# A smooth-quantised stage in halves: column maxima and factor rows read from PSUM, shifts on ScalarE, weights scaled by VectorE, the residual added by GpSimd

## The reference

```python
def _smooth_quant_linear(x, w):
    amax_x = jnp.max(jnp.abs(x), axis=0)
    amax_w = jnp.max(jnp.abs(w), axis=0)
    s = jnp.sqrt(jnp.maximum(amax_x, EPS) / jnp.maximum(amax_w, EPS))
    s = jnp.maximum(s, EPS)
    xs = x / s
    ws = w * s
    x_scale = jnp.maximum(jnp.max(jnp.abs(xs), axis=-1, keepdims=True), EPS) / QMAX
    w_scale = jnp.maximum(jnp.max(jnp.abs(ws), axis=-1, keepdims=True), EPS) / QMAX
    x_q = jnp.clip(jnp.round(xs / x_scale), -QMAX, QMAX)
    w_q = jnp.clip(jnp.round(ws / w_scale), -QMAX, QMAX)
    return x_q @ w_q.T * x_scale * w_scale.T

def _expert_forward(xe, guw, dw):
    h = _smooth_quant_linear(xe, guw)
    gate, up = jnp.split(h, 2, axis=-1)
    a = jax.nn.silu(gate) * up
    return _smooth_quant_linear(a, dw)
```

## Time and profile before

| | us |
|---|---|
| median of 3 runs | 1110.71 |
| lowest, highest | 1105.49, 1112.2 |
| profiled execution, time | 1110.76 |
| profiled execution, span | 1109.0 |
| PE busy in the span | 850.5 (77%) |
| DVE busy | 741.6 (67%) |
| ACT busy | 567.9 (51%) |
| POOL busy | 406.2 (37%) |

### The profile page before, as it was taken

How to read it: one execution, slowest core, us unless ns; L and a number is a source line. 1 busy time by engine, 2 the same in 40 slices (tenths; PEclk the granted TensorE clock), 3 DMA queues, 4 the chain that set the end, 5 groups by cost and what they waited for, 6 DMA issues and landing times. The chain is left out here.

```text
span 1109.0 us, 16326 instructions
## 1 busy us (share of the span) xinstructions
PE 850.5 (77%) x5170; PEld 503.2 (45%) x5170; DVE 741.6 (67%) x1441; ACT 567.9 (51%) x1070; POOL 406.2 (37%) x332
## 2 busy tenths in 40 slices
PE   3356666979899999998597588998539999634477
PEld 1122223642477777776376452332416666422135
DVE  5799996879666676666788557994533333157785
ACT  3433342477677777776474365887304432123162
POOL 0476650047555555553231270000025665202122
PEclk8689998999999999999699597999759999856589
DMA  3222205600000000000000101400572333230001
GB/s 91 78 76 76 76 1 199 219 10 11 10 15 19 19 20 20 14 19 1 5 1 1 52 1 39 135 3 2 201 276 53 74 49 48 28 96 0 0 1 38
DMA packets 44330, 57.61 MB, mean 52 GB/s; under 512 B 5656, under 2 KB 35104, under 8 KB 44272
## 3 DMA queue, kind: packets, MB, share of 16 engines
q1 hardware_dynamic: 37776, 48.72, 13.1%
q0 software_dynamic: 4416, 6.03, 3.3%
q10 hardware_dynamic: 2080, 2.10, 0.5%
HBM read 50.29 MB, written 6.49 MB: 51 GB/s over the span
## 5 line engine op out<-in xcount | busy, mean ns | idle before, releaser
L1225 POOL TENSOR_TENSOR a_scratch<-a_scratch,a_inverse 128x512 f32<-128x512 f32 x64 | 66.6, 1041 | 117.8 <-DVE a_inverse L1357 117.8
L322 PE MATMUL bank<-ssm_seen,ident 128*128 128x512 f32 x128 | 63.6, 621 | 39.0 <-DVE ssm_seen L498 39.0
L424 POOL TENSOR_TENSOR ssm_drive<-ssm_du,ssm_b_row 128x1024 f32<-128x1024 f32 x32 | 75.2, 2352 | 33.4 <-DVE ssm_state L488 33.3
L2204 DVE TENSOR_REDUCE a_tops<-bank 128x4 f32<-128x1024 f32 x64 | 77.6, 1223 | 13.5 <-PE bank L1893 10.7
L2403 PE MATMUL bank<-wup,moe_xT 128*128 x184 | 84.9, 605 | 1.2 <-ACT moe_xT L2461 1.1
L390 ACT ACTIVATE bank<-ssm_delta,ssm_a_neg 128x510 f32<-128x510 f32 x64 | 44.1, 690 | 80.7 <-DVE ssm_state L488 77.7
L2633 DVE TENSOR_TENSOR moe_act_f<-bank,moe_silu 128x512 f32<-128x512 f32 x23 | 15.9, 692 | 96.0 <-ACT moe_silu L2468 84.2
L488 DVE TENSOR_TENSOR_SCAN ssm_state<-bank,ssm_drive 128x512 f32<-128x512 f32 x64 | 74.8, 1210 | 7.6 <-POOL ssm_drive L424 4.9
L2057 ACT ACTIVATE wup<-bank,a_exp_scale 128x1024 f32<-128x1024 f32 x64 | 71.1, 1114 | 16.9 <-PE bank L1916 16.8
L1144 ACT ACTIVATE a_scratch<-bank,a_bias,a_q_factor 128x256 f32<-128x256 f32 x128 | 71.1, 560 | 10.4 <-DVE a_bias L1344 10.1
L969 PE MATMUL bank<-keys,a_scratch 128*128 (+1 forms) x256 | 69.8, 396 | 0.7 <-DVE keys L1282 0.4
(11 more groups left out here) (477 smaller groups left out, 2190.4 us busy)
## 6 DMA issues: line engine op xcount, KB each, us to landing
ssm_b_row<-ssm_b_spill SPq DMA_DIRECT2D x16, 512.0 KB, 3.6
wup<-in_l_up_dram SPq DMA_DIRECT2D x8, 1024.0 KB, 8.6
a_wq_in<-in_l1x_q_dram SPq DMA_DIRECT2D x32, 128.0 KB, 2.1
wdn<-in_l_down_dram SPq DMA_DIRECT2D x8, 512.0 KB, 9.6
keys<-in_l1x_o_dram SPq DMA_DIRECT2D x1, 2048.0 KB, 12.7
X<-in_x_dram SPq DMA_DIRECT2D x1, 1024.0 KB
lora_raw<-in_l_gate_dram SPq DMA_DIRECT2D x1, 1024.0 KB, 8.3
lora_raw<-in_l_up_dram SPq DMA_DIRECT2D x1, 1024.0 KB, 10.3
```

Source lines behind the costliest of these rows:

```text
L322: last = pe.matmul(bank[:, 4 + 2 * k + h, :], core.ident[:, :], seen[:, k, h * HALF:(h + 1) * HALF], start=False, stop=m >= STEPS - CC, sk ...
L424: pool.tensor_tensor(drive[:, k, :], du[:, k, :], b_row[:, n % NROW, :], ALU.mult).then_inc(S["drive_ready"], 1)
L1225: pool.tensor_tensor(prob[:, j, :, :], prob[:, j, :, :], inverse[:, j, :].unsqueeze(2).to_broadcast([P, 2, SEQ]), ALU.mult).then_inc(S["p_ ...
L2204: dve.tensor_reduce(tops[:, f // 2 % 3, :, first:first + 2].rearrange("p q h -> p h q"), bank[:, at:at + 2, :].rearrange("p h (q n) -> p h ...
```

## The change

The whole stage goes by halves of four tiles (`tiles(h)`). The column maxima are read from PSUM, where TensorE turned the activations, and ScalarE no longer makes `xnT`. The spread factor rows are not copied to SBUF: VectorE reads them from PSUM as it multiplies (`rows`). Each spread matmul starts after its own four diagonals. VectorE multiplies the weights too, in place of GpSimd. Multiplying by the inverse scale and adding 1.5 * 2^23 is done by ScalarE, one instruction per tile with two per-partition factors (`shifted`); all roundings to integers are VectorE's, by halves, set between its other steps. The weights' scale row comes in two halves: the first ahead of the turned weights, the second behind products 0 and 1; ScalarE multiplies it by the gate in the second product. Of the first product's turned weights VectorE copies one of the two chunks. Silu, its product, its turning and the second maxima go by halves, and the two table loads of ScalarE are placed by hand. In the second product VectorE writes the rescaled tile to `hidden`, and GpSimd adds it to `X`. In the diff, lines taken out are left out where the listing above has them.

```diff
@@ declarations @@
...
+        shift = s.sb("shift", [P, 1])
-        rows = lambda r, row: row[:, :, :].unsqueeze(2).to_broadcast([P, NB, 2, wide(r)])
+        tiles = lambda h: slice(NT // 2 * h, NT // 2 * (h + 1))
+        def rows(r, first, h):
+            flat = bank[:, first + h, :] if r == 0 else bank[:, first, h * SEQ:(h + 1) * SEQ]
+            return flat.rearrange("p (b n) -> p b n", b=2).unsqueeze(2).to_broadcast([P, 2, 2, wide(r)])
...
@@ -2739,84 +2742,106 @@
             @block.tensor
             def _(pe):
                 s.norm_tensor(pe)
...
+                def spread(r, first, factors, ready, count):
+                    for h in range(CHUNKS[r]):
+                        pe.wait_ge(ready, count + h + 1)
+                        pe.matmul(bank[:, first + h, :], core.ones[:, :], factors[:, 4 * h:4 * h + 4, :],
+                                  start=True, stop=True).then_inc(row_s[r], 1)
+                def turn_ints(r, ints, dst, banks, h):
+                    pe.wait_ge(ints[r], h + 1)
+                    for c in range(CHUNKS[r]):
+                        for t in range(NT // 2 * h, NT // 2 * (h + 1)):
+                            last = pe.transpose(half_bf(banks[r][c])[:, t * P:(t + 1) * P],
+                                                dst[r][:, t, c * P:(c + 1) * P], core.identh[:, :])
+                    return last
+                def scale_row(r, h):
+                    pe.wait_ge(diag_w[r], h + 1)
+                    pe.matmul(bank[:, 2 + h, :], core.ones[:, :], diag[:, 4 * h:4 * h + 4, :], start=True, stop=True
+                              ).then_inc(row_w[r], 1)
+                def multiply(r, t):
+                    if t >= 2:
+                        pe.wait_ge(used[r], t - 1)
+                    for c in range(CHUNKS[r]):
+                        last = pe.matmul(bank[:, t % 2, 0:DM], xqT[r][:, c, t * P:(t + 1) * P],
+                                         wqT[r][:, c, t // 2 * DM:(t // 2 + 1) * DM], start=c == 0, stop=c == CHUNKS[r] - 1)
+                    last.then_inc(product[r], 1)
                 def quantised(r):
                     C = CHUNKS[r]
...
+                    spread(r, 2, diag_inv, diag_s[r], 0)
+                    spread(r, 0, diag, diag_s[r], C)
                     for h in range(2):
...
+                        last = turn_ints(r, x_int, xq, XB, h)
+                    last.then_inc(x_turned[r], 1)
+                    scale_row(r, 0)
+                    for h in range(2):
+                        last = turn_ints(r, w_int, wq, WB, h)
+                    last.then_inc(w_turned[r], 1)
                     pe.wait_ge(x_back[r], 1)
...
+                    pe.wait_ge(w_back[r], C)
+                    multiply(r, 0)
+                    multiply(r, 1)
+                    scale_row(r, 1)
+                    for t in range(2, NT):
+                        multiply(r, t)
                 quantised(0)
...
+                for h in range(2):
+                    pe.wait_ge(a_ready, h + 1)
+                    for t in range(4):
+                        last = pe.transpose(bank[:, 4 + h, t * P:(t + 1) * P], a_nat[:, 4 * h + t, :], core.ident[:, :])
+                    last.then_inc(a_turned, 1)
                 quantised(1)
             @block.scalar
             def _(act):
...
+                s.norm_root(act)
+                def shifted(nat, mult, ready, done, h):
+                    act.wait_ge(ready, h + 1)
+                    for t in range(NT // 2 * h, NT // 2 * (h + 1)):
+                        last = act.activation(nat[:, t, :], nat[:, t, :], ACT.Identity, scale=mult[:, t:t + 1], bias=shift[:, 0:1])
+                    last.then_inc(done, 1)
+                def scale_row(r, h):
+                    act.wait_ge(row_w[r], h + 1)
+                    act.activation(w_scale_row[r][:, h * HALF:(h + 1) * HALF], bank[:, 2 + h, :], ACT.Copy,
+                                   scale=1.0 if r == 0 else gate).then_inc(rowcopy_w[r], 1)
                 def quantised(r):
...
                     act.wait_ge(ratio[r], 1)
                     act.activation(smooth[r][:, :], amax_x[r][:, :], ACT.Sqrt).then_inc(root[r], 1)
...
+                    for h in range(2):
+                        shifted(x_nat[r], x_mult[r], x_scaled[r], x_shifted[r], h)
+                    for h in range(2):
+                        shifted(w_nat[r], w_mult[r], w_scaled[r], w_shifted[r], h)
                     act.wait_ge(x_turned[r], 1)
                     act.copy(xqT[r][:, :, :], half_bf_banks(XB[r])).then_inc(x_back[r], 1)
+                    scale_row(r, 0)
                     act.wait_ge(w_turned[r], 1)
...
+                    act.copy(wqT[r][:, 0, :], half_bf(WB[r][0])).then_inc(w_back[r], 1)
+                    scale_row(r, 1)
                 half_bf_banks = lambda bs: bank[:, bs[0]:bs[-1] + 1, :].bitcast(BF16)
+                act.wait_ge(shift_ready, 1)
                 quantised(0)
...
+                act.preload_act_table_set("silu_and_others")
+                for h in range(2):
+                    act.wait_ge(used[0], NT // 2 * (h + 1))
+                    act.activation(silu[:, tiles(h), :], hidden[:, tiles(h), 0:CTX], ACT.Silu).then_inc(silu_done, 1)
+                act.preload_act_table_set("sqrt_and_others")
                 quantised(1)
             @block.gpsimd
             def _(pool):
...
+                pool.memset(shift[:, :], ROUND).then_inc(shift_ready, 1)
+                for t in range(NT):
+                    pool.wait_ge(used[1], t + 1)
+                    pool.tensor_tensor(core.X[:, t, :], core.X[:, t, :], hidden[:, t, :], ALU.add).then_inc(times, 1)
             @block.vector
             def _(dve):
@@ -2828,69 +2853,82 @@
                     ins.then_inc(step, 1)
                     dve.wait_ge(step, steps[0])
...
+                def diagonals(dst, blocks, column):
+                    for k in blocks:
                         last = dve.tensor_scalar(dst[:, k, :], core.ident[:, :], column(k), None, ALU.mult)
                     return last
...
+                def scale_part(r, first, nat, scale, mult, done, count, h):
+                    dve.wait_ge(row_s[r], count + min(h, CHUNKS[r] - 1) + 1)
+                    chain(dve.tensor_tensor(shape(nat[:, tiles(h), :]), shape(nat[:, tiles(h), :]), rows(r, first, h), ALU.mult))
+                    chain(dve.tensor_reduce(scale[:, tiles(h)], nat[:, tiles(h), :], AX.X, ALU.max, apply_absolute_value=True))
+                    chain(dve.tensor_scalar(scale[:, tiles(h)], scale[:, tiles(h)], EPS, 1.0 / QMAX, ALU.max, ALU.mult))
+                    dve.reciprocal(mult[:, tiles(h)], scale[:, tiles(h)]).then_inc(done, 1)
+                def integers(nat, shifted, dst, done, h):
+                    dve.wait_ge(shifted, h + 1)
+                    dve.tensor_scalar(dst[:, tiles(h), :], nat[:, tiles(h), :], ROUND, QMAX, ALU.subtract, ALU.min).then_inc(done, 1)
+                def quantised(r):
                     C = CHUNKS[r]
...
                     chain(dve.tensor_scalar(amax_x[r][:, :], amax_x[r][:, :], EPS, None, ALU.max))
                     dve.tensor_tensor(amax_x[r][:, :], amax_x[r][:, :], amax_w[r][:, :], ALU.mult).then_inc(ratio[r], 1)
                     dve.wait_ge(root[r], 1)
                     chain(dve.tensor_scalar(smooth[r][:, :], smooth[r][:, :], EPS, None, ALU.max))
...
                     chain(dve.reciprocal(inverse[r][:, :], smooth[r][:, :]))
                     at = lambda k: slice((k % C) * NB + k // C, (k % C) * NB + k // C + 1)
...
+                    for dst, values in ((diag_inv, inverse[r]), (diag, smooth[r])):
+                        for h in range(C):
+                            diagonals(dst, range(4 * h, 4 * h + 4), lambda k: values[:, at(k)]).then_inc(diag_s[r], 1)
+                    x = lambda h: scale_part(r, 2, x_nat[r], x_scale[r], x_mult[r], x_scaled[r], 0, h)
+                    w = lambda h: scale_part(r, 0, w_nat[r], w_scale[r], w_mult[r], w_scaled[r], C, h)
+                    x(0)
+                    x(1)
+                    dve.wait_ge((w_in, c_in)[r], 16)
+                    w(0)
+                    integers(x_nat[r], x_shifted[r], xq[r], x_int[r], 0)
+                    w(1)
+                    integers(x_nat[r], x_shifted[r], xq[r], x_int[r], 1)
+                    dve.wait_ge(w_scaled[r], 2)
+                    for h in range(2):
+                        diagonals(diag, range(4 * h, 4 * h + 4), lambda k: w_scale[r][:, k:k + 1]).then_inc(diag_w[r], 1)
+                        integers(w_nat[r], w_shifted[r], wq[r], w_int[r], h)
+                    if C == 2:
+                        dve.wait_ge(w_turned[r], 1)
+                        dve.tensor_copy(wqT[r][:, 1, :], half_bf(WB[r][1])).then_inc(w_back[r], 1)
+                def rescale(r, t):
                     dve.wait_ge(product[r], t + 1)
...
+                    dve.wait_ge(rowcopy_w[r], t // 4 + 1)
```

(23 more changed lines are left out.)

110 lines of the change are left out of this document (5 added, 105 removed).

## The result

The changed kernel takes 1097.22 us (median of 4, 1093.48 to 1104.49) against 1110.38 us; the ratio of its runs to those of before is 0.9886, 95% interval 0.9841 to 0.9931. Timed again twice it came to 0.9861 (0.9819 to 0.9903) and 0.9853 (0.9826 to 0.9879). Over all series of runs, 16 executions of it have a mean of 1096.4 us and 56 of the kernel before 1111.0 us: 14.6 us less, with a standard error of 1.1. The kernel before timed against itself gave 1.0018 (0.9996 to 1.0039). The forecast was 1097.8 us.

What follows compares the result with a forecast made beforehand. VectorE was taken to lead the last stage, its idle quarter being hand-offs between engines. Gains 1.94, 6.47, 2.1, 4.0 and 0.45 less a 2.0 loss summed to 13.0 us, from 1110.76 to 1097.8 us; range 1092 to 1105.

Steps and rivals of the forecast that it cites:

- maxima from PSUM: First product: four VectorE maxima read PSUM directly, ending at 985.07 us where the maximum ended at 987.01; gain 1.94 us.
- to the first rescaling: First product, from the maxima's end to its first rescaling: 23.93 us where it was 30.40; gain 6.47 us.
- to the second rescaling: Second product, from its maxima's end to its first rescaling: 17.75 us where it was 21.76; gain 4.0 us.
- tail: Second product's rescalings and residual additions: 6.95 us where they took 7.40, GpSimd adding at 0.70 us a tile; gain 0.45.
- Halves: VectorE's scaling steps by halves: 2.93 us per half of 1024 columns, 1.87 per half in the second product.
- The waits on GpSimd: First product: VectorE's 2.36 us instruction on 8 numbers, ending with GpSimd's weight multiplication, goes once VectorE multiplies the weights.
- Shifts on ScalarE at no cost: Scale-and-shift steps in both products: 0.56 us each, beside VectorE; cost nothing, cover 0.8 us in the first product.
- The added wait on TensorE: Rescalings after the second wait for the scale row's second half: 2.0 us lost in the first product, 1.1 at 2.4 GHz.
- A: ScalarE's scale-and-shift steps are late, at double price 1.1 us each: gain 9.6 us, time 1101.2 us; chance 0.12.
- B: GpSimd's additions in the tail cost 1.2 us each: tail grows by 3.0, gain 10.0, time 1100.8 us; chance 0.10.
- D: Slower: GpSimd and VectorE shut each other out in the tail; 1123 us at 4.0 us per addition; chance 0.05.
- C: Halves double the hand-offs, TensorE stays at 1.2 GHz through both tails: gain 10 us, time 1100.8 us; chance 0.09.

Runs made afterwards that it cites:

- third trace: The changed kernel timed and profiled again with no edits, beside the kernel before: ratio 0.9853, stage 65.30 us.
- first trace: First profile of the changed kernel, against the kernel before: median 1097.22 us, ratio 0.9886, stage 62.57 us.

## Why the prediction was right, point by point

The time was right within 0.6 us, but part of that is luck: the stage saved 4.7 us more than the sum in that trace, and the way to it took 5.2 us longer. The sum of 13.0 us was made for TensorE at 1.2 GHz. The third trace of the changed kernel is that case, and there the stage saves 14.95 us (80.25 less 65.30); at 2.4 GHz, in the first two, 17.7. The means of all executions are 14.6 us apart with a standard error of 1.1. That fits the 14.95 well and the 17.7 badly; the mean of the three traces is 16.8, and whether the 2 us between are scatter outside the stage or a small loss stays open.

| step | predicted | 1.2 GHz (third trace) | 2.4 GHz (first trace) |
|---|---|---|---|
| maxima from PSUM | 1.94 | 2.10 | 2.11 |
| to the first rescaling | 6.47 | 6.94 | 7.89 |
| rescalings, second scale row behind product 1 | -2.0 | -1.62 | -0.32 |
| between the products | 2.1 | 2.35 | 2.81 |
| to the second rescaling | 4.0 | 4.63 | 4.64 |
| tail | 0.45 | 0.57 | 0.57 |

- **Maxima.** Right; the second pair began a little earlier than I had it.
- **Halves.** A half of 1024 columns took 2.80 us (997.50 less 994.70, the starts of two halves' multiplications), not 2.93, and one of 512 columns 1.75, not 1.87: the next half starts before the last small instruction ends. Over eight halves that is 1.0 us, about what the ways to the two rescalings saved beyond the sum at 1.2 GHz (0.47 and 0.63). One thing went the other way: ScalarE's root in the first product starts 0.37 us after its input (990.50 to 990.87), where it took 0.03 before. In the second product it is 0.04, though its maxima are read from PSUM too, so that reading isn't the cause; none is shown.
- **The waits on GpSimd.** Shown: with the weights put back on it, the instruction on four numbers took 4.00 us and ended with GpSimd's. On the path this is worth 1.3 us, since VectorE then has the two multiplications less. By the page SBUF — State Buffer of the Trainium skill, the part on the engine side's ports, an instruction of VectorE in a two-port mode or with two SBUF inputs and one of GpSimd exclude each other for a whole instruction. The 4.00 us agree, if that instruction ran in such a mode, which no trace shows. VectorE's two additions in the tail, with two SBUF inputs, agree (0.9 us each where a multiplication of 512 columns takes 0.68), and so do its rescalings, with one, which kept their 0.48 us beside GpSimd's additions.
- **Shifts on ScalarE at no cost.** Right. Each took 0.59 us (0.56 from the earlier trace rows), from start to start 0.50, and VectorE never waited. Put back on VectorE they cost 3.4 to 4.4 and 2.8 us on the path.
- **The added wait on TensorE.** Right in place and mechanism, and in size at the level it was worked out for: the gap is 1.65 us at 1.2 GHz, where I wrote "some 1.5 us" (1.25 in the second product), and 0.42 at 2.4. The six rescalings behind it took 2.85 us, not the 3.25 of the sum. I had named the other level, for 0.9 us, but left it out of the sum. It is the largest single miss of the sum, 1.7 us in the traces at 2.4 GHz.
- **The tail.** GpSimd's addition cost 0.68 to 0.69 from start to start, 0.70 predicted. With the additions on VectorE the tail is 0.89 longer, so the move pays though GpSimd is the slower engine, by 0.69 to 0.48. The Trainium skill, GPSIMD Engine Reference, section Engine selection, has GpSimd about 2x slower with two inputs and would leave such work on VectorE. The ratio here is 1.4, and following the advice was 0.89 us dearer: GpSimd had nothing else to do. But once the scale row is out of the way, GpSimd is what the tail waits for.
- **What a measurement shows.** "What this stage saves reaches the end" holds: the last stage took 52.67 us before and 52.86 after. The 5.2 us ahead of the stage in the first pair of traces go with the granted clock in the attention stage, 0.72 and 0.50 in the stretch shown; a fixed loss of that size is out.
- **Rivals.** A, B and D are out by the prices above; C is out, as the halves cost less than summed and the stage saved at least 14.95 us, not 10, with TensorE at 1.2 GHz at both products' ends.

## What to carry to other kernels

Add up a short dependent stage at both levels of TensorE's clock and keep both sums; the same program got either level at the same point in different executions. When a chain of engines is the bound, work that moves to an idle engine pays even at a worse price, but look next at whether that engine has become the last to finish. And compare stages from trace to trace, not only times: here the stage before repeated to 0.2 us while the executions of its kernel lay between 1102.6 and 1117.4.
